# Flamingo gated block: another order of the first loads, of GpSimd's constants and of the first normalisation

## The chip, the cores and the metric

The kernel runs on one core of one Trainium2 chip. The metric is the device time of one execution in microseconds (us). The core has five engines that run their own instruction streams and meet in semaphores: TensorE (PE, with its weight loads PEld), VectorE (DVE), ScalarE (ACT), GpSimd (POOL) and SyncE (SP), which here only issues transfers. Transfers run on 16 DMA engines. SP's transfers are on queue q1, ACT's on queue q10.

## The reference

`x` is 32 batches of 56 tokens of 128 features; `ctx` is 32 batches of 1500 context rows of 128 features.

```python
x = x + tanh(g_xattn) * xattn(layernorm(x), ctx)     # 16 heads of depth 8, biases on q, k, v, o
x = x + tanh(g_ffn)   * ffn(layernorm(x))            # 160 experts, top 8 of sigmoid(logits), plus one shared

# xattn: q = xn@Wq.T+bq; k = ctx@Wk.T+bk; v = ctx@Wv.T+bv
#        out = softmax(q.k/sqrt(8)) @ v, per head;  out @ Wo.T + bo
# ffn:   p = sigmoid(xn@router.T + bias); top 8, normalised to sum 2.5
#        sum over experts of  silu(xn@w_gate[e].T) * weight[e] @ w_down[e].T
```

## The kernel before

**Attention.** Tokens are kept as `xt` [112, 16, 128]: two batches side by side on the partitions, 16 such pairs. The pairs fall in four groups of 448 tokens (`TC`); `FIRST` is the first group (pairs 0 to 3), `REST` the three others. Context rows of one batch are `ctx_in[:, u]` with 125 partitions of 12 rows, in three chunks of four tiles (`NCH = 3`); `u` is the batch's parity. For each chunk GpSimd makes a high and a low fp16 part (`split_ctx`, lines 563 and 565), SP issues a DMA transpose into `ctT` (line 377), PE makes the keys from it in three products (lines 1298 for batch 0, 1401 for the others), ACT writes the high part of the keys (733, 858) and DVE the low part (982, 1160). GpSimd builds from the queries `q_hi` a block matrix `q_blk` (line 663). PE multiplies it with the keys in 21 products a batch, which only give the row maxima (line 1377; DVE reduces each, line 1030; three PSUM banks hold them, so a product must wait for the maximum two places before it). The scores themselves come from stacked rows, `k_stk` and `q_st` (line 1358), ACT takes their exponential (line 800) and PE multiplies them with the values (line 1343).

**Steps.** `attention()` runs `body(step)` for each step on each engine; a body has 12 places k = 0 to 11. In step s the keys of batch s, the maxima and values of batch s-1 and the scores of batch s-2 are made. Keys come at k = 2, 6, 10 on PE, and one place later on ACT and DVE; values at k = 0, 4, 8 on PE and at k = 1, 5, 9 on ACT. Scores begin at k = 3. So step 1 has the maxima of batch 0 and the keys of batch 1, and step 2 has the first scores. Steps 0 to 3 are written out, the rest is a loop. What stands aside of this is put at places by tables such as `SCALE_REST_AT = (1, 3)` (step 1, k = 3), called by `aside`.

**Aside work that the change touches.** The layernorm of `FIRST` is made before step 1: DVE centres (`centre`, lines 953 to 955), ACT squares (709) and takes roots (718), DVE scales (967, 968), PE transposes four pairs (1277), ACT copies (723), PE multiplies with `wqT` (1292), ACT writes `q_hi` (728), DVE `q_lo` (976). The layernorm of `REST`: DVE `centre(*REST)` (953 to 955) before step 1, ACT `square_rest` (739), DVE variance (1005, `VAR_REST_AT`), ACT root (718), DVE reciprocal (1010, `RSTD_REST_AT`), ACT `scale_rest` (745, `SCALE_REST_AT`), then tokens (`TOKENS_REST_AT`), query products (`Q_REST_AT`), `q_hi` (`Q_HI_REST_AT`) and `q_lo` (`Q_LO_REST_AT`). The 16 rows of Wo, `output_rows`, are copied by 16 transfers that ACT issues in fours (line 789, `OUT_ROWS_AT`).

**Start.** SP issues the first tokens (line 330), chunk 0 of batch 0 (325), the four weights Wq, Wk, Wv, Wo (347), chunks 1 and 2. ACT issues the padding rows (749), three biases (752), the remaining tokens (330) and the rows of batch 1 (325). PE may begin with the transposes of the weights (1273) when all four are there; ACT copies these (761). After the three transposes of batch 0, SP has in its stream: load of batch 2, eight issues of `stack_queries` (369, after `q_hi` and `q_lo`), transpose of chunk 0 of batch 1, four issues more, chunks 1 and 2 of batch 1, `stack_keys` of batch 0 (405, 12 issues). GpSimd waits for the padding and splits the three chunks of batch 0, then makes its constants (608 to 617), then `q_blk`.

**FFN.** After attention a loop over 80 expert pairs runs on PE, ACT and DVE (lines 1540, 1550, 867, 874, 1203, 1210). The change touches nothing there.

Of the kernel before, what the change touches and what calls it, by code (L numbers as in the profile page):

```python
# [14 lines left out]
def flamingo_gated_block(nc, x, ctx, g_xattn, g_ffn, Wq, bq, Wk, bk, Wv, bv, Wo, bo,  # L15
# [53 lines left out]
    FIRST, REST = (0, PPC), (PPC, NP)  # L69
    VAR_REST_AT, RSTD_REST_AT, SCALE_REST_AT = (1, 1), (1, 2), (1, 3)  # L70
    TOKENS_REST_AT = {(1, 5): (1, 3), (1, 8): (3, 4)}
    Q_REST_AT = {(1, 6): (1, 3), (1, 9): (3, 4)}
    Q_HI_REST_AT = {(1, 7): (1, 3), (1, 10): (3, 4)}
    Q_LO_REST_AT = {(1, 8): (1, 3), (1, 11): (3, 4)}
    SHARED_AT, GATES_AT, CONSTANT_AT, QUERIES_FREE_AT, OUT_FREE_AT = (2, 0), (2, 1), (2, 2), (2, 1), (2, 4)
    OUT_ROWS_AT = {(1, 4): 0, (1, 6): 4, (1, 8): 8, (1, 10): 12}
    AGGR_AT = (B - 2, 2)
# [12 lines left out]
    with stk:  # L90
# [236 lines left out]
        def load_x(eng, p0, p1, here):  # L327

            for b in range(2):
                eng.dma_start(xt[b * T:(b + 1) * T, p0:p1, :],  # L330
                              x.rearrange("(n b) t c -> b t n c", b=2)[b, :, p0:p1, :]).then_inc(here, 16)
# [7 lines left out]
        def _(sp):  # L339
            def load_chunk(c):  # L340
                j = slice(c * TPC, (c + 1) * TPC)
                load_rows(sp, first_here[c], ctx_in[0:KP, 0, j, :], ctx[0].rearrange("(p j) c -> p j c", j=KT)[:, j, :])

            load_x(sp, *FIRST, x_in)
            load_chunk(0)
            for n, w in enumerate((Wq, Wk, Wv, Wo)):
                sp.dma_start(w_raw[:, n, :], w).then_inc(weights_in, 16)
            for c in range(1, NCH):
                load_chunk(c)
# [171 lines left out]
        def _(pool):  # L521
            made = [0]

            def const(ins):

                made[0] += 1
                ins.then_inc(consts, 1)
                pool.wait_ge(consts, made[0])
# [75 lines left out]

            pool.wait_ge(pad_here, 32)
            for c in range(NCH):
                split_ctx((0, 0), c)
            const(pool.memset(den_spread[:, :], 0.0))
# [5 lines left out]
            const(pool.memset(k_stk[96:97, 0, 0, :], 1.0))  # L614
            assert made[0] == K_ONES
            const(pool.memset(v_sb[:, :, :, 0:4, 3 * d:VW], 1.0))
            const(pool.memset(v_sb[:, :, :, 4:VG, d:VW], 1.0))
# [88 lines left out]
        def _(act):  # L706
# [41 lines left out]
            for u in range(2):  # L748
                act.dma_start(ctx_in[KP:128, u, :, :], ctx[0].rearrange("(p j) c -> p j c", j=KT)[0:128 - KP, :, :])\
                   .then_inc(pad_here, 16)  # L750
            for dst, src in ((bqc, bq), (bkc, bk), (bvc, bv)):
                act.dma_start(dst[:, :], src.rearrange("(p a) -> p a", a=1)).then_inc(bias_in, 16)
            load_x(act, *REST, x_rest)
            load_rows(act, ctx_here[1], ctx_in[0:KP, 1, :, :], ctx[1].rearrange("(p j) c -> p j c", j=KT))
            act.wait_ge(o_cleared, 2)
            load_root_table(1, sq_first[:, 0, 0:1], ones_d[0:PT, 0:1])
            square(1, sq_first, *FIRST)

            for n, w in enumerate((wqT, wk_hi, wv_hi, woT)):
# [178 lines left out]
        def _(dve):  # L938
# [53 lines left out]
            scale(1, *FIRST)  # L992
            dve.wait_ge(x_rest, 32)
            centre(*REST)
            dve.wait_ge(bias_in, 16 * 3)
            dve.wait_ge(bqs_made, 1)
            queries(0, 1)
            for c in range(NCH):
                first_keys(c)
            dve.wait_ge(o_cleared, 2)  # L1000
            v.tensor_scalar(bv_rep[:, :], ones_d[:, :], bvc[:, 0:1], None, ALU.mult).then_inc(bv_made, 1)
# [652 lines left out]
```

## Time and profile before

| | us |
|---|---|
| three runs | 1126.83, 1124.95, 1122.03 |
| median | 1124.95 |
| the profiled execution, its own time | 1124.83 |
| its span | 1123.2 |
| PE busy in the span | 1068.0 |
| DVE busy | 963.5 |
| ACT busy | 847.6 |
| GpSimd busy | 591.7 |

The mean granted clock of TensorE is 0.99 of full speed. The span counts from the first to the last instruction. PE is busy for 95% of it, except in its first 40th, 28 us, where it is busy for two tenths. The change touches the first 60 us alone.

### The profile page before, as it was taken

The page shows a single profiled execution, that of the slowest core. Times are in us where ns is not written, and L with a number is a line of the kernel's source. Part 1 is how long each engine was busy: PE and PEld are TensorE (multiplying, and loading weights), DVE is VectorE, ACT ScalarE, POOL GpSimd, SP SyncE. Part 2 cuts the span into 40 slices and gives each one's busy share as a digit, 9 for nine tenths or more (in the row PEclk, how much of TensorE's full clock was granted, in tenths as well). Part 3 has the DMA queues.
Part 4 walks back from the last instruction along what each step waited for, and adds up shares of the span by engine and source line. Part 5 has one row for each costly group of instructions (what it writes and reads, how often), then busy time and mean ns, then how long its engine had stood idle before and what let it go on. Part 6 is the DMA issues. An engine that isn't in the chain of part 4 may idle for free.

```text
span 1123.2 us, 37415 instructions
## 1 busy us (share of the span) xinstructions
PE 1068.0 (95%) x12142; PEld 708.1 (63%) x12142; DVE 963.5 (86%) x1699; ACT 847.6 (75%) x1817; POOL 591.7 (53%) x984
## 2 busy tenths in 40 slices
PE   2799999999999999999999999998999999999998
PEld 1366777777777777777777777654455555555554
DVE  4678888888888888888888888578999999999998
ACT  3476777777777777777777776687888888888887
POOL 5798887887888888788888886320000000000000
PEclk9799999999999999999999999999999999999999
DMA  8778777577577576676676652482788778777873
GB/s 159 158 166 214 145 178 179 123 184 170 133 186 170 131 186 162 142 185 152 152 185 142 150 132 67 110 207 97 229 228 226 226 236 237 229 229 227 230 237 118
DMA packets 229501, 197.12 MB, mean 175 GB/s; under 512 B 161039, under 2 KB 207263, under 8 KB 229462
## 3 DMA queue, kind: packets, MB, share of 16 engines
q1 hardware_dynamic: 218036, 173.22, 61.8%
q0 software_dynamic: 9200, 21.85, 6.9%
q10 hardware_dynamic: 2226, 1.56, 0.7%
q8 instruction: 21, 0.34, 0.1%
q14 instruction: 18, 0.15, 0.0%
HBM read 109.96 MB, written 12.55 MB: 109 GB/s over the span
## 4 chain that ended last, share of the span: by engine, by line
PE 75%; DVE 12%; issue 4%; SPq 3%; ACT 2%; DMA 2%; DVEq 0%; POOL 0%; ACTq 0%
PE bank L1550 15%; PE bank L1540 15%; PE bank L1343 12%; PE bank L1377 11%; PE bank L1358 10%; DVE part_max L1030 6%; PE bank L1413 5%; PE bank L1401 4%; DVE rec L1169 2%; PE bank L1457 1%; SPq L369 1%; DMA ctx_in<-in_ctx_dram 1%; SPq L405 1%; DVE o_raw L1044 1%; DVE kparts L1160 1%
## 5 line engine op out<-in xcount | busy, mean ns | idle before, releaser
L800 ACT ACTIVATE p_exp<-bank 125x448 f32<-125x448 f32 x768 | 400.1, 544 | 183.9 <-PE bank L1358 182.9
L1030 DVE TENSOR_REDUCE part_max<-bank 128x1 f32<-128x500 f32 x672 | 420.1, 671 | 62.0 <-PE bank L1377 61.5
L1358 PE MATMUL bank<-q_st,k_stk 97*125 97x224 f16 x1536 | 272.6, 261 | 2.5 <-ACT p_exp L800 1.9
L1377 PE MATMUL bank<-kparts,q_blk 128*128 128x500 f16 x672 | 255.8, 384 | 17.5 <-DVE part_max L1030 13.2
L1358 PEld LDWEIGHTS bank<-q_st,k_stk 97*125 97x125 f16 x1536 | 195.9, 138 | 66.2 <-ACT p_exp L800 13.1
L867 ACT ACTIVATE ctT<-bank 128x448 f32<-128x448 f32 x320 | 174.2, 545 | 40.9 <-DVE v_sb L1203 9.8
L1210 DVE TENSOR_TENSOR ctT<-v_sb,ctT 128x448 f16<-128x448 f32 (+1 forms) x324 | 200.4, 619 | 0.2
L1550 PE MATMUL bank<-ctT,w_ring 128*128 128x448 f16 x816 | 198.9, 352 | 0.1
L874 ACT ACTIVATE ctT<-v_sb 128x448 f16<-128x448 f32 x320 | 182.2, 569 | 7.0 <-DVE v_sb L1203 6.9
L1343 PE MATMUL bank<-p_exp,v_sb 125*25 125x168 f32 (+1 forms) x6144 | 186.2, 262 | 0.4 <-ACT p_exp L800 0.4
L1343 PEld LDWEIGHTS bank<-p_exp,v_sb 125*25 125x25 f32 x6144 | 142.1, 103 | 42.6 <-ACT p_exp L800 0.5
L1540 PE MATMUL bank<-q_hi,w_ring 128*128 128x448 f16 x544 | 147.3, 352 | 0.0
L1550 PEld LDWEIGHTS bank<-ctT,w_ring 128*128 128x128 f16 x816 | 79.7, 98 | 74.6 <-DVE ctT L1210 3.5
L565 POOL TENSOR_TENSOR ctx_parts<-ctx_in,ctx_parts 128x512 f16<-128x512 f32 x96 | 111.2, 1159 | 8.0
L1203 DVE TENSOR_TENSOR v_sb<-v_sb,ctT 128x448 f32<-128x448 f32 x154 | 95.8, 622 | 6.9 <-ACT ctT L867 2.6
L1203 DVE TENSOR_TENSOR v_sb<-k_stk,ctT 128x448 f32<-128x448 f32 x154 | 96.0, 624 | 5.6 <-issue 2.5
L1160 DVE SCALAR_TENSOR_TENSOR kparts<-bank,bkc,kparts 128x500 f16<-128x500 f32 x93 | 68.0, 731 | 38.0 <-ACT kparts L858 38.0
L1540 PE MATMUL bank<-q_lo,w_ring 128*128 128x448 f16 x272 | 95.9, 352 | 0.0
L1377 PEld LDWEIGHTS bank<-kparts,q_blk 128*128 128x128 f16 x672 | 64.9, 97 | 44.2 <-DVE part_max L1030 23.5
L1540 PEld LDWEIGHTS bank<-q_hi,w_ring 128*128 128x128 f16 x544 | 53.2, 98 | 49.7
L1413 PE MATMUL bank<-wv_hi,ctT 128*125 128x128 f16 x768 | 84.0, 224 | 0.0
L1413 PEld LDWEIGHTS bank<-wv_hi,ctT 128*125 128x125 f16 x768 | 77.7, 140 | 2.8 <-issue 2.8
(193 smaller groups left out, 1376.3 us busy)
## 6 DMA issues: line engine op xcount, KB each, us to landing
k_stk<-kparts SPq DMA_DIRECT2D x384, 93.8 KB, 4.1
v_sb<-c_scratch SPq DMA_DIRECT2D x68, 448.0 KB, 4.3
k_stk<-c_scratch SPq DMA_DIRECT2D x68, 448.0 KB, 4.3
ctx_in<-in_ctx_dram SPq DMA_DIRECT2D x30, 672.0 KB
w_scratch<-w_out POOLq DMA_DIRECT2D x80, 128.0 KB, 3.2
w_in<-in_L_ffn_w_gate_dram POOLq DMA_DIRECT2D x80, 64.0 KB, 3.7
w_in<-in_L_ffn_w_down_dram POOLq DMA_DIRECT2D x80, 64.0 KB, 4.1
v_sb<-c_scratch SPq DMA_DIRECT2D x8, 336.0 KB, 3.8
```

The source lines that it names most:

```text
L800: act.activation(p_exp[0:KP, j % PR, f * 448:(f + 1) * 448], ST[f][0:KP, 0:448], ACT.Exp).then_inc(exp_done, 1)
L867: act.activation(s_act[:, (r - 1) % 2 if isinstance(r, int) else z % 2, :], ZB[z][:, 0:TC], ACT.Silu)\
L874: act.activation(h_hi[:, b, :], h_f[:, b, :], ACT.Copy).then_inc(hh_done, 1)
L1030: v.reduce_max(part_max[:, i // NCH, i % NCH:i % NCH + 1], SM[i % NSM][:, 0:CK], axis=AX.X).then_inc(sm_maxed, 1)
L1203: v.tensor_tensor(h_f[:, b, :], c, s_act[:, (r - 1) % 2 if isinstance(r, int) else b % 2, :], ALU.mult).then_inc(h_done, 1)
L1210: v.tensor_tensor(h_lo[0:rows, b, :], h_f[0:rows, b, :], h_hi[0:rows, b, :], ALU.subtract).then_inc(hl_done, 1)
L1343: last = pe.matmul(OB[32 * (g % 4):32 * (g % 4) + VW, at:at + w], v_sb[0:KP, u, j, g, 0:VW], p_exp[0:KP, j % PR, src:src + w], start=(j == ...
L1358: last = pe.matmul(ST[f][0:KP, (g % 2) * GC:(g % 2 + 1) * GC], k_stk[0:97, u, g, j * KP:(j + 1) * KP], q_st[0:97, u, g, :, :].rearrange("p ...
L1377: pe.matmul(SM[i % NSM][:, 0:CK], rows, kparts[:, u, 0, c * CK:(c + 1) * CK], start=True, stop=True).then_inc(sm_done, 1)
L1413: last = pe.matmul(VB[0:KP, i * D:(i + 1) * D], ctT[:, u, c, part, i, 0:KP], w[:, :], start=(n == 0), stop=(n == 2))
L1540: last = pe.matmul(ZB[z][:, 0:TC], w[:, a, :], xparts[b][:, t * TC:(t + 1) * TC], start=(j == 0), stop=(j == 2))
L1550: last = pe.matmul(YB[t][:, 0:TC], part, hparts[b][rows, at, :], start=(shared and i == 0), stop=(end and i == 2), skip_group_check=True)
```

## The change

The weights are issued by ACT after the padding, in place of SP between chunks 0 and 1. ACT issues the remaining tokens and batch 1 behind `square(1, ...)`, no longer ahead of the table load. GpSimd makes `den_spread` and the ones of `k_stk` ahead of its wait for the padding; the two fills of `v_sb` stay behind the splits. DVE centres `REST` behind the first keys. The tables move the rest of that layernorm by three places, and the output rows to other places.

```diff
-    VAR_REST_AT, RSTD_REST_AT, SCALE_REST_AT = (1, 1), (1, 2), (1, 3)
-    TOKENS_REST_AT = {(1, 5): (1, 3), (1, 8): (3, 4)}
...
+    VAR_REST_AT, RSTD_REST_AT, SCALE_REST_AT = (1, 4), (1, 5), (1, 6)
+    TOKENS_REST_AT = {(1, 8): (1, 3), (1, 11): (3, 4)}
...
-    OUT_ROWS_AT = {(1, 4): 0, (1, 6): 4, (1, 8): 8, (1, 10): 12}
+    OUT_ROWS_AT = {(1, 1): 0, (1, 4): 4, (2, 0): 8, (2, 2): 12}
...
             load_x(sp, *FIRST, x_in)
-            load_chunk(0)
-            for n, w in enumerate((Wq, Wk, Wv, Wo)):
-                sp.dma_start(w_raw[:, n, :], w).then_inc(weights_in, 16)
-            for c in range(1, NCH):
+            for c in range(NCH):
                 load_chunk(c)
...
-            pool.wait_ge(pad_here, 32)
-            for c in range(NCH):
-                split_ctx((0, 0), c)
             const(pool.memset(den_spread[:, :], 0.0))
...
             const(pool.memset(k_stk[96:97, 0, 0, :], 1.0))
             assert made[0] == K_ONES
+            pool.wait_ge(pad_here, 32)
+            for c in range(NCH):
+                split_ctx((0, 0), c)
...
+            for n, w in enumerate((Wq, Wk, Wv, Wo)):
+                act.dma_start(w_raw[:, n, :], w).then_inc(weights_in, 16)
             for dst, src in ((bqc, bq), (bkc, bk), (bvc, bv)):
...
-            load_x(act, *REST, x_rest)
-            load_rows(act, ctx_here[1], ctx_in[0:KP, 1, :, :], ctx[1].rearrange("(p j) c -> p j c", j=KT))
             act.wait_ge(o_cleared, 2)
             load_root_table(1, sq_first[:, 0, 0:1], ones_d[0:PT, 0:1])
             square(1, sq_first, *FIRST)
+            load_x(act, *REST, x_rest)
+            load_rows(act, ctx_here[1], ctx_in[0:KP, 1, :, :], ctx[1].rearrange("(p j) c -> p j c", j=KT))
...
             scale(1, *FIRST)
-            dve.wait_ge(x_rest, 32)
-            centre(*REST)
...
             for c in range(NCH):
                 first_keys(c)
+            dve.wait_ge(x_rest, 32)
+            centre(*REST)
```

The tables of the query products move likewise: `Q_REST_AT` from (1, 6) and (1, 9) to (1, 9) and (2, 0), `Q_HI_REST_AT` from (1, 7) and (1, 10) to (1, 10) and (2, 0), `Q_LO_REST_AT` from (1, 8) and (1, 11) to (1, 11) and (2, 1). PE's wait `QUERIES_FREE_AT` goes from (2, 1) to (2, 2).

VectorE's stream before, from the scaling of the first tokens to the first maxima of step 1:

```order
L968 TENSOR_TENSOR xc<-xc,stat 112x512
L953 TENSOR_REDUCE stat<-xt 112x12
L954 TENSOR_SCALAR stat<-stat 112x12
L955 TENSOR_TENSOR xc<-xt,stat 112x1536
L976 SCALAR_TENSOR_TENSOR q_lo<-bank,bqs,q_hi 128x448
L982 SCALAR_TENSOR_TENSOR kparts<-bank,bkc,kparts 128x500 x3
L1001 TENSOR_SCALAR bv_rep<-ones_d,bvc 128x112
L1030 TENSOR_REDUCE part_max<-bank 128x1 x4
```

The same place in the changed kernel:

```order
L967 TENSOR_TENSOR xc<-xc,stat 112x512
L975 SCALAR_TENSOR_TENSOR q_lo<-bank,bqs,q_hi 128x448
L981 SCALAR_TENSOR_TENSOR kparts<-bank,bkc,kparts 128x500 x3
L952 TENSOR_REDUCE stat<-xt 112x12
L953 TENSOR_SCALAR stat<-stat 112x12
L954 TENSOR_TENSOR xc<-xt,stat 112x1536
L1000 TENSOR_SCALAR bv_rep<-ones_d,bvc 128x112
L1029 TENSOR_REDUCE part_max<-bank 128x1 x8
```

The three centring instructions of `REST` stand now between the last low part of the keys and the first maximum.

ScalarE's stream before, from the last keys of step 1 backwards and forwards to the first exponential (`xnT` are copies of tokens, `wo_m` the output rows):

```order
L789 DMA wo_m<-woT 8x128 x4
L834 ACTIVATE v_sb<-bank 125x4x4x24
L836 ACTIVATE v_sb<-bank 125x4x4x8
L728 ACTIVATE q_hi<-bank,bqs 128x448
L789 DMA wo_m<-woT 8x128 x4
L858 ACTIVATE kparts<-bank,bkc 128x500
L847 ACTIVATE neg_row<-bank 7x128
L834 ACTIVATE v_sb<-bank 125x4x4x24
L836 ACTIVATE v_sb<-bank 125x4x4x8
L776 ACT_TABLE_LOAD
L776 ACTIVATE tg<-g_raw 112x2
```

The same stretch in the changed kernel, from the last keys of step 1:

```order
L857 ACTIVATE kparts<-bank,bkc 128x500
L720 ACTIVATE xnT<-bank 128x448
L846 ACTIVATE neg_row<-bank 7x128
L725 ACTIVATE q_hi<-bank,bqs 128x448
L788 DMA wo_m<-woT 8x128 x4
L833 ACTIVATE v_sb<-bank 125x4x4x24
L835 ACTIVATE v_sb<-bank 125x4x4x8
L775 ACT_TABLE_LOAD
L775 ACTIVATE tg<-g_raw 112x2
L778 ACTIVATE sg<-bank 128x64
```

Eight of the output rows' issues leave step 1 for step 2, four of them right behind the last `q_hi` and four between the table load and the first exponential.

## Rows read from the trace of the kernel before

**Rows 1.** Chain of waits, first 110 us: start us, us, what.

```profile
6.37 12.10 DMA ctx_in<-in_ctx_dram
...
28.90 3.79 DMA ctT<-ctx_parts
...
75.27 0.79 SPq L413
```

**Rows 2.** Issues: source, queue, count, KB each, us to landing, for Wo.

```profile
w_raw<-in_L_xattn_Wo_dram SPq DMA_DIRECT2D x1, 64.0 KB, 7.7
```

**Rows 3.** Timeline of ScalarE: start us, us, instruction, idle before it.

```profile
4.38 1.28 ACTq L325 DMA_DIRECT2D ctx_in<-in_ctx_dram  x2
5.69 1.28 ACT L713 ACT_TABLE_LOAD   x1 [5.69 <-issue]
...
12.48 0.28 ACT L761 ACTIVATE wqT<-bank 128x128 f32<-128x128 f32 x1 [4.62 <-PE bank L1273]
...
22.04 0.63 ACT L728 ACTIVATE q_hi<-bank,bqs 128x448 f16<-128x448 f32 x1 [0.88 <-PE bank L1292]
...
47.12 2.72 ACTq L789 DMA_DIRECT2D wo_m<-woT  x4
49.89 0.49 ACT L834 ACTIVATE v_sb<-bank 125x384 f32<-125x384 f32 x1 [2.28 <-issue]
...
52.69 0.68 ACT L858 ACTIVATE kparts<-bank,bkc 128x500 f16<-128x500 f32 x1 [1.62 <-issue]
...
56.45 1.28 ACT L776 ACT_TABLE_LOAD   x1
...
60.25 0.54 ACT L800 ACTIVATE p_exp<-bank 125x448 f32<-125x448 f32 x1 [1.84 <-PE bank L1358]
```

**Rows 4.** Timeline of GpSimd.

```profile
5.99 0.61 POOL L563 CAST ctx_parts<-ctx_in 128x512 f16<-128x512 f32 x1 [2.44 <-DMA ctx_in<-in_ctx_dram]
...
25.31 1.68 POOL L663 TENSOR_TENSOR q_blk<-q_hi,head_mask 128x896 f16<-128x896 f16 x1
26.93 0.61 POOL L563 CAST ctx_parts<-ctx_in 128x512 f16<-128x512 f32 x1
...
28.72 0.61 POOL L563 CAST ctx_parts<-ctx_in 128x512 f16<-128x512 f32 x1
```

**Rows 5.** Timeline of SP's issues.

```profile
23.71 2.55 SPq L369 DMA_DIRECT2D q_stk<-q_hi  x4
```

**Rows 6.** Timeline of TensorE.

```profile
19.02 0.60 PE L1298 MATMUL bank<-ctT,wk_hi 128*128 128x500 f16 x1 [3.47 <-DMA ctT<-ctx_parts]
...
53.47 0.99 PE L1377 MATMUL bank<-kparts,q_blk 128*128 128x500 f16 x2 [2.49 <-issue]
```

**Rows 7.** Windows: busy of PE, PEld, DVE, ACT, POOL; granted clock, DMA share, GB/s.

```profile
4.00:6.00 2.00, 0.00 (x0) 0.00 (x0) 1.45 (x3) 0.31 (x1) 0.01 (x1) 1.00 0.54 135
...
8.00:10.00 2.00, 0.00 (x0) 0.00 (x0) 0.74 (x2) 0.00 (x0) 0.00 (x0) 1.00 1.18 201
...
44.00:46.00 2.00, 0.06 (x1) 0.00 (x0) 2.00 (x5) 0.02 (x1) 2.00 (x4) 1.00 0.51 156
46.00:48.00 2.00, 1.94 (x7) 1.25 (x8) 1.02 (x2) 0.54 (x1) 2.00 (x4) 0.52 0.61 171
```

**Rows 8.** Timeline of VectorE.

```profile
15.33 1.75 DVE L953 TENSOR_REDUCE stat<-xt 112x12 f32<-112x1536 f32 x1 [0.91 <-DMA xt<-in_x_dram]
...
17.83 1.76 DVE L955 TENSOR_TENSOR xc<-xt,stat 112x1536 f32<-112x1536 f32 x1
```

**Rows 9.** Groups by line, 26 to 53 us, VectorE: busy us, mean ns, idle before.

```profile
L1030 DVE TENSOR_REDUCE part_max<-bank 128x1 f32<-128x500 f32 x21 | 13.2, 672 | 7.8 <-PE bank L1377 7.8
```

**Rows 10.** Groups by line, 30 to 60 us, ScalarE.

```profile
L745 ACT ACTIVATE xc<-xc,stat 112x128 f32<-112x128 f32 x12 | 3.6, 390 | 0.0
```

**Rows 11.** Groups by line, 44 to 52 us, TensorE.

```profile
L1292 PE MATMUL bank<-xnT,wqT 128*128 128x448 f32 x2 | 1.9, 1034 | 0.0
...
L1277 PE MATMUL bank<-ident,xc 112*128 112x112 f32 x4 | 1.0, 398 | 2.0 <-DVE q_lo L976 2.0
```

More of the change, by code:

```diff
@@ L69, in flamingo_gated_block @@
     FIRST, REST = (0, PPC), (PPC, NP)
-    VAR_REST_AT, RSTD_REST_AT, SCALE_REST_AT = (1, 1), (1, 2), (1, 3)
-    TOKENS_REST_AT = {(1, 5): (1, 3), (1, 8): (3, 4)}
[L72 to L75, printed above, removed]
-    OUT_ROWS_AT = {(1, 4): 0, (1, 6): 4, (1, 8): 8, (1, 10): 12}
+    VAR_REST_AT, RSTD_REST_AT, SCALE_REST_AT = (1, 4), (1, 5), (1, 6)
+    TOKENS_REST_AT = {(1, 8): (1, 3), (1, 11): (3, 4)}
+    Q_REST_AT = {(1, 9): (1, 3), (2, 0): (3, 4)}
+    Q_HI_REST_AT = {(1, 10): (1, 3), (2, 0): (3, 4)}
+    Q_LO_REST_AT = {(1, 11): (1, 3), (2, 1): (3, 4)}
+    SHARED_AT, GATES_AT, CONSTANT_AT, QUERIES_FREE_AT, OUT_FREE_AT = (2, 0), (2, 1), (2, 2), (2, 2), (2, 4)
+    OUT_ROWS_AT = {(1, 1): 0, (1, 4): 4, (2, 0): 8, (2, 2): 12}
     AGGR_AT = (B - 2, 2)
```

## The prediction, made before the changed kernel was run

> **What bounds the kernel now.** I read the chain of waits of the first 110 us, then the timelines of the engines over 60 us, then windows of 2 us for the clock and the transfers. PE is busy for 95% of the span, so most of the time can't be touched here; but in the first 28 us it is busy for a fifth. There the chain is one transfer, 12.10 us long [rows 1]: the last chunk of batch 0, behind weights, other tokens and batch 1. TensorE's first keys start at 19.02, after 3.47 us of waiting for the transpose [rows 6], which lay in SP's queue behind all chunks. `q_hi` of the first group ends at 22.04 + 0.63 = 22.67 [rows 3]. From there SP issues eight stacks of queries (23.71 on, 0.64 each) and at 28.90 the transpose of batch 1's chunk 0, which lands 3.79 later, at 32.7 [rows 1, 5]. GpSimd begins `q_blk` only at 25.31, though `q_hi` is there 2.6 us before [rows 4]: its constants are in the way. Step 2 starts on PE at 53.47, after 2.49 us without a wait that the profile shows [rows 6]; ScalarE's last keys were late, as its engine sat idle 1.62 us while its stream issued four output rows, and 2.28 us before that [rows 3]. The first exponential starts at 60.25 [rows 3]. From there the work is bound by PE, SP's row of maxima follows at 75.27 [rows 1] and all that comes later hangs on it. So I follow one quantity: how much earlier than 60.25 the first exponential starts. Nothing behind it is changed, and I count that gain one for one in the span.
>
> **The start.** What is needed first is 224 KB of tokens, 768 KB of batch 0 with its padding and 256 KB of weights, 1.28 MB. Data flow from about 2 us, at 135 GB/s in 4:6 and 201 in 8:10 [rows 7]; my sum over the windows puts 1.28 MB at 8.6 to 8.8 (all earlier tokens and rows of batch 1 are out of the way). The weights are the last of it or ahead: Wo landed 7.7 us after its issue [rows 2], near 11.9; now at 8.6. PE's transposes take about 1.1, ACT's copies begin at 9.75 in place of 12.48 [rows 3]. ACT has by then issued the four transfers that move behind `square`: the table load stays within 0.6 of its 5.69 [rows 3] (four weights' issues come ahead of it, four others go), the square ends near 7.3, issues of 2.3 us (1.28 for batch 1's two [rows 3], 1.0 for the tokens) run from 6.9 to 9.2, free. The normalised first tokens are 2.7 earlier, at 12.85 on PE. The transpose of chunk 0 is issued as now at about 7.9, since the split starts at 5.99 [rows 4] after chunk 0's landing, and with 3.79 to land is there at 11.7; a bound on the other side is 13. The first keys start at 12.85 in place of 19.02, and `q_hi` ends 3.65 later as now, at 16.5: 6.2 earlier. GpSimd's early constants fit in the 2.44 us for which it waits now [rows 4]; if chunk 0 lands before they are done, they cost at most 0.5. A split takes 1.79 (26.93 to 28.72 [rows 4]), so the third ends at 11.4, its transpose lands at 15.2 to 16.4, and the third low part of the keys ends near 18.7.
>
> **What takes the place.** (a) `centre(*REST)` now stands between the keys and the maxima: 15.33 to 19.59, 4.26 us [rows 8]. First maximum at 23.3. Six maxima at 13.2/21 = 0.63 [rows 9] end at 27; PE's keys at k = 2 need only the fourth, 25.1. So the centring, once hidden behind the wait for the transfer, is hidden again, behind SP. (b) SP: 16.5 plus 5.2 of issues is 21.7. But batch 1 must be here and split: its rows and the other tokens are 1.45 MB and begin to flow at 9.2; at 201 GB/s [rows 7] that is 16.4, and three transposes of 0.25 MB each beside it make it 20.2. Split 1.79, transpose at 22.0, landing at 25.85 in place of 32.7: 6.8 earlier. The bounds of the landing are 25.5 (SP alone) and, below as a rival, 29 or more.
>
> (c) Step 1 behind that. Before: 32.7 to 53.47, 20.8 us. Now ScalarE's work comes in series, since the scaling of `REST` is at k = 6 behind the second four output rows. The terms: keys of batch 1 1.45; two maxima, a low part, two maxima, variance and root 3.6; four issues 2.72 (the stream of ScalarE is held, as the 2.28 of idle shows [rows 3]), behind which stand values, scaling and the second keys; values 0.75; scaling 3.6 [rows 10]. VectorE waits for the second keys then, and PE stands idle for some 2.7 us. An idle of 2 us in 44:46 is followed by a granted clock of 0.52, the lower level, in 46:48 [rows 7], so I take the tokens at 1.0 a group and the first query product at 1.9 [rows 11]: two groups of tokens 2.0; maxima between 0.9; queries 1.9 and 0.9; last maximum and keys 0.9; ACT's keys 0.7; low parts 0.7 and 0.6; the last tokens 0.9. Sum 21.6, so step 2 starts at 47.45, 6.0 earlier. The old idle from the output rows ahead of the last keys is gone, but the serial scaling and the clock eat it.
>
> (d) Head of step 2. Before: 53.47 to 60.25, 6.8. Now two maxima and the values 2.2; the last query product, which moved in here, 1.9 at the lower clock (0.9 at the higher); then ACT, in order: `q_hi` and four issues 2.7, values 0.75, to 55.0; the table load (1.28, begun at 56.45 before [rows 3]) with its copies, and beside it four more issues, 2.1 more. First exponential at 57.1 in place of 60.25. VectorE's constant term waits for the same copies and stays beside it. That costs 2.9 of the 6.0: eight output rows stand where the first scores are wanted. If the clock is at its higher level here, 1.2 less.
>
> The sum: 6.8 gained up to the landing, 0.8 lost in step 1, 2.9 lost in the head of step 2: 3.1 to 3.2 earlier. The profiled execution took 1124.83, and the median of the runs shown is 1124.95, the same within 0.1. Forecast 1121.6. Its own range is 1119.8 (higher clock in both places, SP's bound) to 1123.
>
> SP's and GpSimd's streams keep up: SP reaches the row of maxima of batch 0 near 48, 6 to 7 earlier than at present, and the scores want it at 54.
>
> **Rivals.**
> 1. The whole gain of the head survives. The output rows' issues have cost idle time before as well, and if PE keeps its higher clock (in 44:46 it was still 1.00 [rows 7]) and ScalarE issues the last four beside its queued work, step 2 starts at 46 and the first exponential is bound by PE's scores alone, 6.8 to 7.5 later: 53.3, 6.9 gained, 1117.9. Against: the 2.28 and 1.62 of idle [rows 3] say the issues do hold the engine.
> 2. Batch 1 comes last; this is the way to slower. SP loads batch 2 (0.77 MB) right behind the third transpose, at 12.7, beside ACT's queue. If the 16 engines serve the two in turn, 1.45 + 0.75 + 0.77 = 2.97 MB must pass: at 201 GB/s to 24.0, at 135 [rows 7] to 31. It decides from 20.0 on, and each microsecond later is one lost on GpSimd's split, SP's transpose and everything queued behind it. At 24.0: 3.8 more, 1125.4; at 26, 1127.4; at 31, 1132. For it: the twelve-microsecond transfer of [rows 1] was such a mixture. Against: 2.7 MB passed by 16 us in the kernel before.
> 3. The weights don't come earlier: behind another queue Wo may again take until 11.9 [rows 2], since batch 0's three chunks now run beside them. Then copies at 12.5 and all from the first keys on is 2.7 later: 1124.3. This is also how the change would not do what it says.
>
> On rival 2 the Trainium skill speaks. "DMA: Bandwidth & Descriptors", section "Queues, rings and completion order", says that each DMA engine takes turns between the queues with work, a packet at a time, and its section "Issuing engines are not separate DMA queues" that issuing from two engines saves only issue time. By that rule batch 1 would share evenly with batch 2 from about 14.7 and land near 22.5; the sum would be 2.3 us less gain, 1123.9. The trace agrees as far as it shows it, for q10's tokens were issued by 4.4 and landed only at 15.33, beside q1's weights and chunks.
>
> **How the numbers follow.** Forecast 0.48; rival 1 0.27; rival 2 0.15; rival 3 0.10. Range: 1117.0, below rival 1, to 1125.6, which takes in rivals 3 and the milder half of 2; about 0.1 is left above and 0.08 below. A measurement of this kernel can tell some 0.5%, 5.6 us, from no change. Faster by more than that is below 1119.3: rival 1 nearly whole and a little of the forecast, 0.31. Slower by more is above 1130.6: only the far end of rival 2, 0.05. Within: 0.64.
>
> **What would show it.** ACT's weight copies near 9.8 and `q_hi` ending near 16.5 (rival 3: 19). The first maximum on VectorE near 23.3, behind the centring. The first wait for keys in step 1 ending at 25 to 26 (rival 2: GpSimd waits for batch 1's rows beyond 20). Step 2 at 47 to 48. ScalarE idle for "issue" ahead of the first exponential, which starts at 57 (rival 1: 53), and a granted clock near 0.5 ahead of it. The prediction is wrong if the span behind the first exponential, 1123.2 less 60.25, should become longer or shorter by more than 1 us.

## The result, and the profile after

The changed kernel took 1130.11 us, the median of 7 runs (1127.82 to 1149.86), against 1124.06 of the kernel before (7 runs, 1122.03 to 1127.24). The run of 1149.86 had a lower granted clock than the six others (0.941 against 0.988 to 0.991), so the ratio leaves it out; the median of the six is 1129.06. The ratio is 1.0048, with a 95% interval of 1.0027 to 1.0069: slower by about half a per cent, some 5 us. The forecast was 1121.6, its range 1117.0 to 1125.6; the time lies outside it, on the slow side.

The profiled execution took 1132.42, with a span of 1130.9, 7.7 more than before. It was the slowest of the six, so the losses read from it are some 2 us larger than those of the medians. Four marks in the two traces say where it went. The first is the start of the first keys of batch 1 on TensorE, the second the start of step 2, the third the first exponential, the fourth SP's row of maxima [rows 1].

| mark | before | forecast | after |
| --- | --- | --- | --- |
| first keys of batch 1 | 32.7 | 25.85 | 32.08 |
| step 2 | 53.47 | 47.45 | 53.47 |
| first exponential | 60.25 | 57.1 | 64.64 |
| SP's next row of maxima | 75.27 | | 81.60 |
| end of the span | 1123.2 | | 1130.9 |

So 0.7 us were gained up to batch 1, lost again in step 1, 4.4 were lost in the head of step 2, 1.9 in the 15 us behind the first exponential, and 1.4 in the thousand behind those. TensorE's timeline of the changed kernel (start us, us, instruction, idle ahead of it in brackets) answers to [rows 6]:

```profile
8.23 1.09 PE L1272 MATMUL bank<-ident,w_raw 128*128 128x128 f32 x4 [8.23 <-DMA w_raw<-in_L_xattn_Wo_dram]
...
17.50 0.60 PE L1297 MATMUL bank<-ctT,wk_hi 128*128 128x500 f16 x1 [5.33 <-DMA ctT<-ctx_parts]
...
30.52 1.77 PE L1376 MATMUL bank<-kparts,q_blk 128*128 128x500 f16 x3 [4.53 <-DVE part_max L1029]
32.08 0.62 PE L1400 MATMUL bank<-ctT,wk_hi 128*128 128x500 f16 x1
...
44.22 1.76 PE L1276 MATMUL bank<-ident,xc 112*128 112x112 f32 x8 [2.58 <-ACT xc L742]
...
53.47 1.04 PE L1376 MATMUL bank<-kparts,q_blk 128*128 128x500 f16 x2
...
60.19 0.38 PE L1357 MATMUL bank<-q_st,k_stk 97*125 97x224 f16 x2 [0.20 <-issue]
...
65.23 0.63 PE L1357 MATMUL bank<-q_st,k_stk 97*125 97x224 f16 x2 [4.04 <-ACT p_exp L799]
```

The weights are earlier, as forecast (8.23). The first keys are only 1.5 us earlier than before, behind a wait of 5.33 for the transpose. At 30.52 TensorE waits for VectorE's maxima, no longer for a transfer. And the first scores of step 2 are ready near 60.6 but ScalarE takes them at 64.64; from 65.2 to 69.7 the matmuls that took 0.38 at 60.19 take about 0.6. The chain of waits (start, us, what) shows the new head, in answer to [rows 1]:

```profile
8.24 9.21 DMA ctT<-ctx_parts
17.50 1.43 PE bank L1297 x3
18.93 1.51 PE bank L1291 x2
20.52 0.64 ACT q_hi L725
```

One transfer of 12.10 us has been replaced by a transpose of 9.21. It is the first of batch 0's three; why it is so long, e4 and e9 show. VectorE's timeline, in answer to [rows 8]:

```profile
24.27 1.74 DVE L952 TENSOR_REDUCE stat<-xt 112x12 f32<-112x1536 f32 x1
26.05 0.54 DVE L953 TENSOR_SCALAR stat<-stat 112x12 f32<-112x12 f32 x1
26.62 2.10 DVE L954 TENSOR_TENSOR xc<-xt,stat 112x1536 f32<-112x1536 f32 x1
28.65 1.22 DVE L1000 TENSOR_SCALAR bv_rep<-ones_d,bvc 128x112 f32<-128x112 f32 x1
29.80 3.59 DVE L1029 TENSOR_REDUCE part_max<-bank 128x1 f32<-128x500 f32 x6
...
44.76 0.74 DVE L1159 SCALAR_TENSOR_TENSOR kparts<-bank,bkc,kparts 128x500 f16<-128x500 f32 x1 [3.93 <-ACT kparts L857]
```

The centring stands ahead of the first maximum without a gap, and that maximum is at 29.80. Later VectorE waits 3.93 for keys that ScalarE gives late. ScalarE's timeline says why, in answer to [rows 3]:

```profile
8.77 0.28 ACT L760 ACTIVATE wqT<-bank 128x128 f32<-128x128 f32 x1 [1.32 <-PE bank L1272]
...
20.52 0.63 ACT L725 ACTIVATE q_hi<-bank,bqs 128x448 f16<-128x448 f32 x1 [0.88 <-PE bank L1291]
...
37.34 2.63 ACTq L788 DMA_DIRECT2D wo_m<-woT  x4
40.02 0.49 ACT L833 ACTIVATE v_sb<-bank 125x384 f32<-125x384 f32 x1 [2.53 <-issue]
...
40.56 3.60 ACT L742 ACTIVATE xc<-xc,stat 112x128 f32<-112x128 f32 x12
44.06 0.66 ACT L857 ACTIVATE kparts<-bank,bkc 128x500 f16<-128x500 f32 x1
...
57.26 2.62 ACTq L788 DMA_DIRECT2D wo_m<-woT  x4
59.93 0.49 ACT L833 ACTIVATE v_sb<-bank 125x384 f32<-125x384 f32 x1 [2.09 <-issue]
...
60.60 1.28 ACT L775 ACT_TABLE_LOAD   x1
...
64.64 0.54 ACT L799 ACTIVATE p_exp<-bank 125x448 f32<-125x448 f32 x1 [2.08 <-issue]
```

Four issues, then twelve scalings, then the keys: the series that the new tables set up. In the head of step 2 the engine idles 2.09 and 2.08 us while its stream issues eight output rows, the second time with the scores waiting.

### The profile page after: what moved, and what is told of

Read it like the earlier page. It is cut to its first block, busy times and chain, and to the rows that moved or that the text cites. A ratio compares the mean times of both kernels' runs of the same rounds, so it can differ in the third digit from the quotient of the medians.

```text
span 1130.9 us, 37415 instructions
## 1 busy us (share of the span) xinstructions
PE 1071.3 (95%) x12142; PEld 709.8 (63%) x12142; DVE 965.9 (85%) x1699; ACT 847.8 (75%) x1817; POOL 593.7 (52%) x984
## 3 DMA queue, kind: packets, MB, share of 16 engines
q1 hardware_dynamic: 217460, 172.96, 60.6%
## 4 chain that ended last, share of the span: by engine, by line
PE 68%; DVE 15%; issue 6%; SPq 3%; POOL 3%; DMA 2%; ACT 2%; DVEq 1%; ACTq 0%; POOLq 0%
PE bank L1549 15%; PE bank L1539 15%; PE bank L1342 10%; PE bank L1357 9%; PE bank L1376 8%; DVE part_max L1029 8%; PE bank L1412 4%; DVE rec L1168 4%; PE bank L1400 3%; PE bank L1456 1%; SPq L402 1%; DMA ctT<-ctx_parts 1%; DVE o_raw L1043 1%; POOL ctx_parts L562 1%; DVE kparts L1159 1%
## 5 line engine op out<-in xcount | busy, mean ns | idle before, releaser
L1376 PE MATMUL bank<-kparts,q_blk 128*128 128x500 f16 x672 | 255.9, 383 | 20.3 <-DVE part_max L1029 18.7
```

The source lines that it names most:

```text
L1376: pe.matmul(SM[i % NSM][:, 0:CK], rows, kparts[:, u, 0, c * CK:(c + 1) * CK], start=True, stop=True).then_inc(sm_done, 1)
```

## The experiments

Each kernel was timed with the kernel before on the same chip; e1 to e4, e5 to e8 and e9 to e11 are three such groups, and across groups the ratios compare better than the medians. Keys, maximum, exponential and row are starts in the profiled execution: first keys on TensorE, first maximum on VectorE, first exponential, and SP's row at 75.27 before.

| kernel | median us | ratio to before, 95% | keys | maximum | exponential | row |
| --- | --- | --- | --- | --- | --- | --- |
| before | 1124.06 | 1 | 19.02 | 27.68 | 60.25 | 75.27 |
| changed | 1130.11 | 1.0048 [1.0027, 1.0069] | 17.50 | 29.80 | 64.64 | 81.60 |
| e1 | 1127.85 | 1.0033 [1.0020, 1.0046] | 17.61 | 29.90 | 62.37 | 78.00 |
| e2 | 1121.83 | 0.9979 [0.9969, 0.9989] | 17.10 | 24.41 | 56.86 | 71.87 |
| e3 | 1124.60 | 1.0003 [0.9990, 1.0016] | 18.14 | 28.05 | 58.70 | 73.72 |
| e4 | 1132.85 | 1.0081 [1.0060, 1.0101] | 11.72 | 33.63 | 67.50 | 84.36 |
| e5 | 1127.54 | 1.0032 [1.0017, 1.0047] | 17.35 | 24.63 | 60.27 | 77.42 |
| e6 | 1125.74 | 1.0017 [1.0006, 1.0027] | 17.46 | 24.72 | 60.15 | 77.62 |
| e7 | 1121.27 | 0.9974 [0.9961, 0.9986] | 17.39 | 24.86 | 56.37 | 71.39 |
| e8 | 1121.79 | 0.9974 [0.9962, 0.9985] | 17.13 | 24.41 | 56.85 | 72.39 |
| e9 | 1120.00 | 0.9965 [0.9952, 0.9977] | 14.43 | 21.68 | 54.17 | 69.72 |
| e10 | 1122.25 | 0.9982 [0.9968, 0.9996] | 17.22 | 26.28 | 56.33 | 71.35 |
| e11 | 1121.94 | 0.9982 [0.9970, 0.9994] | 14.43 | 23.90 | 53.55 | 68.93 |

**e1: the changed kernel with the output rows issued where they were.**

```diff
-    OUT_ROWS_AT = {(1, 1): 0, (1, 4): 4, (2, 0): 8, (2, 2): 12}
+    OUT_ROWS_AT = {(1, 4): 0, (1, 6): 4, (1, 8): 8, (1, 10): 12}
```

> The changed kernel with the 16 output rows at their old places (1, 4), (1, 6), (1, 8), (1, 10). Theory A (the issues of the output rows stand in front of the first exponentials of step 2, ScalarE idle 2.09 and 2.08 us for issue, PE idle 4.04 and then at half clock): the first exponential starts 3 to 4.5 us earlier than in the changed kernel (60 to 61.5 in place of 64.64), PE no longer drops to half clock behind it, total 1124 to 1126. Rival B (the loss is made in step 1, by the centring ahead of the maxima and the serial scaling; the rows only fill slack): the first exponential moves by under 1.5 us, since the issues in step 1 delay the keys there as much, total 1128 to 1131.

The first exponential comes 2.3 us earlier than in the changed kernel, bound by TensorE and not by issues; ScalarE's timeline in this kernel:

```profile
62.37 0.54 ACT L799 ACTIVATE p_exp<-bank 125x448 f32<-125x448 f32 x1 [0.26 <-PE bank L1357]
```

In time the difference is smaller and not clear of noise: the ratios 1.0048 and 1.0033 are 1.7 us apart, and e1's lies within the interval of the changed kernel. If it is real, the eight rows in the head of step 2 account for about a third of the loss; most of the loss is elsewhere.

**e2, e3, e7: the parts of the change that touch no table.** e2 is the kernel before with the new order of loads only, e3 with GpSimd's constants ahead of the splits only, e7 with both.

```diff
 # e2: in the kernel before
             load_x(sp, *FIRST, x_in)
-            load_chunk(0)
-            for n, w in enumerate((Wq, Wk, Wv, Wo)):
-                sp.dma_start(w_raw[:, n, :], w).then_inc(weights_in, 16)
-            for c in range(1, NCH):
+            for c in range(NCH):
                 load_chunk(c)
...
             square(1, sq_first, *FIRST)
+            load_x(act, *REST, x_rest)
+            load_rows(act, ctx_here[1], ...)
```

> The kernel before with only the new order of the loads (weights on ACT's queue, other tokens and batch 1 issued behind the square); centring, tables and GpSimd's constants as before. Theory A (the loads gain what they can, and the moved work costs it): the centring lies in VectorE's idle time ahead of the first keys, the first keys start near 17.5 as in the changed kernel, first maximum near 24.5 to 25.5 in place of 27.7, first exponential 1.5 to 3 us earlier than 60.25, total 1121 to 1123. Rival C (the loads themselves are the harm, as the transposes of batch 0 now share the DMA engines with batch 1): transposes and the keys of batch 1 come later than before, total 1126 or more.

> The kernel before with only GpSimd's constants (den_spread, ones of k_stk) ahead of its wait. Theory A: q_blk starts near 23.2 in place of 25.31, the first maximum is then bound by the third keys at 26, so 1.0 to 1.5 us earlier; the keys of batch 1 still wait for SP until 32.7, so the first exponential and the total move by 0 to 0.5: 1123.5 to 1124.5. Rival D (GpSimd is on the path in the start): 1.5 to 2.5 us earlier.

> The kernel before with the new loads and GpSimd's early constants; centring, tables, output rows as before. The run with the loads alone gave 1121.83. GpSimd finished the splits at 12.1 in the changed kernel and q_hi came at 21.2, so the constants are hidden there in either place: both theories expect no difference, 1121.3 to 1122.3; a gain over 1 us would say that GpSimd is on the path.

The loads alone make the kernel faster, 0.9979, with the interval below 1; the constants alone do nothing measurable (1.0003), and beside the loads they add nothing that the intervals part (0.9974). The loads are worth 2.4 to 3 us; the loss is in what came with them. e3's exponential is 1.5 us earlier than the kernel before's without a difference in the medians. Most likely that is how far one profiled execution scatters in this head (e3's took 1.1 us less than its median), so a difference of that size between two traces shows nothing.

**e6, e5: the changed kernel without the later centring, and with or without the new output rows.** e6 puts both back, so that it is e7 with the changed tables (variance, root, scaling, tokens and queries of the rest three places later); e5 puts back the centring alone. The edit of the centring is shown; that of the rows is e1's.

```diff
 # e5 and e6
+            dve.wait_ge(x_rest, 32)
+            centre(*REST)
             dve.wait_ge(bias_in, 16 * 3)
             dve.wait_ge(bqs_made, 1)
             queries(0, 1)
             for c in range(NCH):
                 first_keys(c)
-            dve.wait_ge(x_rest, 32)
-            centre(*REST)
```

> The changed kernel with centre(*REST) back at its place before, ahead of the first keys; tables and output rows as changed. Theory G (the centring ahead of the first maximum is the largest part of the loss): the first maximum starts near 24.5 in place of 29.80; but the tables still put ScalarE's scaling at k = 6 behind four issues, so the first exponential is 2 to 4 us earlier than 64.64, total 1125 to 1128. Rival H (step 1 is set by the serial chain of the tables and SP, the centring lies beside it): under 1 us, total 1129 to 1131.

> The changed kernel with centre(*REST) and the output rows back; only the tables of the remaining layernorm stay moved by three places. If the three costs add (tables, centring, output rows), this is what the tables alone cost over the kernel with new loads and constants: theory G expects 1123 to 1124.5, that is 1 to 3 us above that kernel; rival H expects 1125 to 1127, the tables being the larger part.

The tables are the largest loss: e6 is 4.5 us above e7 in the medians (intervals 1.0006 to 1.0027 and 0.9961 to 0.9986), and its first exponential is 3.8 later though batch 1's keys start at the same time in both (29.45 and 29.39). ScalarE's timeline of e6:

```profile
35.41 0.21 ACT L715 ACTIVATE stat<-stat 112x12 f32<-112x12 f32 x1 [3.82 <-DVE stat L1004]
35.48 3.10 ACTq L788 DMA_DIRECT2D wo_m<-woT  x4
38.63 0.49 ACT L833 ACTIVATE v_sb<-bank 125x384 f32<-125x384 f32 x1 [3.00 <-issue]
```

and TensorE's:

```profile
42.83 1.76 PE L1276 MATMUL bank<-ident,xc 112*128 112x112 f32 x8 [2.58 <-ACT xc L742]
...
52.59 0.98 PE L1276 MATMUL bank<-ident,xc 112*128 112x112 f32 x4 [4.03 <-DVE q_lo L975]
```

The root waits for a late variance, the values wait for four issues, the tokens for the scaling; the first tokens of the rest come at 42.83, against 34.70 in e7, and the last at 52.59 against 42.32. Nothing is left ahead of the scores to hide that.

Why the old places cost less shows in ScalarE's timeline of the kernel before:

```profile
34.97 0.76 ACTq L789 DMA_DIRECT2D wo_m<-woT  x1
35.07 0.97 ACT L745 ACTIVATE xc<-xc,stat 112x128 f32<-112x128 f32 x3
```

There four issues, from 34.97 to 37.72, stand right behind the twelve scalings. The stream has gone ahead to the issues while the engine still works through the scalings, which take 3.6 us (34.78 to 38.37) as without any issue beside them. With the changed tables the four issues at (1, 4) stand ahead of the scalings, behind a short root alone, and the engine idles 2.53 us (changed kernel) or 3.00 (e6) for them.

The centring costs e1 against e6 1.8 us by the ratios, 1.0033 against 1.0017; the two intervals overlap a little, so the traces must carry it: the first maximum is 5.2 later, batch 1's first keys 2.7 (32.18 and 29.45), the first exponential 2.2. The same edit with the new rows, e5 against the changed kernel, has the first maximum 5.2 and the exponential 4.4 apart, and again overlapping ratios, 1.0032 and 1.0048. The output rows (e5 against e6) change the medians by 1.8, with overlapping intervals, and in the traces the first exponential not at all. They only change what it waits for, as TensorE's timeline of e5 shows:

```profile
55.84 0.38 PE L1357 MATMUL bank<-q_st,k_stk 97*125 97x224 f16 x2 [0.20 <-issue]
...
60.86 0.63 PE L1357 MATMUL bank<-q_st,k_stk 97*125 97x224 f16 x2 [4.03 <-ACT p_exp L799]
```

Step 1 without the last eight rows is shorter, the scores are there 3.9 us before e6's, and ScalarE then takes them at 60.27 all the same, since it issues the eight rows first. With the early centring the issues are paid in the one place or in the other.

**e4: the changed kernel with batch 1 and the other tokens held back until the first tokens are on ScalarE (about 12 us).**

```diff
-            load_x(act, *REST, x_rest)
-            load_rows(act, ctx_here[1], ...)
...
             query_tokens(0, 1)
+            load_rows(act, ctx_here[1], ...)
+            load_x(act, *REST, x_rest)
             first_keys(0)
```

> The changed kernel with batch 1's rows and then the other tokens issued by ACT behind the first tokens' copy (near 12.8 us in place of 6.8 to 8.7). Theory E (the first transpose took 9.2 us to land, from 8.24, because those 1.45 MB pass the same DMA engines beside it): it lands within 3 to 4.5 us, first keys at 12.3 to 13, q_hi ends near 16; but batch 1 is here only at 22 to 25 and the centring waits for the other tokens, so the total is open, 1122 to 1132. Rival F (the first transposes are slow by themselves so early, whatever runs beside them): it lands near 17.4 again and the keys start no earlier than 17.

This is the experiment on the first transpose. TensorE's timeline:

```profile
11.72 0.60 PE L1297 MATMUL bank<-ctT,wk_hi 128*128 128x500 f16 x1
...
21.46 0.60 PE L1297 MATMUL bank<-ctT,wk_hi 128*128 128x500 f16 x1 [5.89 <-DMA ctT<-ctx_parts]
```

Issued at 8.51, the first transpose is there by 11.72, with no wait shown: at most 3.2 us, where the changed kernel's took 9.2. The windows of the two kernels (busy of PE, PEld, DVE, ACT, POOL; granted clock, DMA share, GB/s) show what lay beside it. First e4:

```profile
8.00:10.00 2.00, 1.04 (x4) 0.64 (x4) 1.40 (x6) 1.10 (x6) 1.92 (x3) 1.00 0.09 17
```

then the changed kernel:

```profile
8.00:10.00 2.00, 1.09 (x4) 0.71 (x4) 1.40 (x6) 1.04 (x6) 1.92 (x4) 1.00 0.86 217
10.00:12.00 2.00, 0.81 (x4) 0.66 (x4) 1.04 (x1) 0.00 (x0) 1.92 (x2) 1.00 1.16 177
```

The engines were free for it in e4 and full of the other tokens and batch 1 in the changed kernel. But the kernel is slower, 1.0081: the held loads then lie beside the third transpose (the wait of 5.89 at 21.46), and the other tokens arrive only at 27.57, so the centring and with it the first maximum, at 33.63, come later still. Contention is moved, not taken away.

**e8, e9: on top of e7, output rows in ScalarE's idle time; then batch 1 issued by SP behind batch 0's transposes.**

```diff
 # e8, in e7
-    OUT_ROWS_AT = {(1, 4): 0, (1, 6): 4, (1, 8): 8, (1, 10): 12}
+    OUT_ROWS_AT = {(1, 1): 8, (1, 4): 12}
...
             query_tokens(0, 1)
+            output_rows(0, 8)
             first_keys(0)
 # e9, in e8
-            load_rows(act, ctx_here[1], ...)
...
+            load_rows(sp, ctx_here[1], ...)
             load_ctx((0, 0))
```

> New loads and early constants, centring and tables as before, and the output rows where ScalarE waits anyway: eight issues behind the first tokens' copy (12.9 us, ahead of a wait of some 5.7 us for the first keys), four at (1, 1), four at (1, 4). Theory A (an issue in ScalarE's stream costs time where work is queued behind it): the idle 'issue' of 2.2, 2.8 and 1.6 us in step 1 is gone, step 2 starts 1.6 to 3 us earlier than with the loads alone, total 1119 to 1120.5. Rival I (step 1 is bound by SP and VectorE, ScalarE's idle time costs nothing): no gain, 1121.5 to 1122.3.

> The kernel with output rows in ScalarE's idle time, and batch 1's rows issued by SP behind the three transposes of batch 0, so that only the other tokens (0.69 MB) pass beside the first transpose. Theory E: the first transpose lands in 5 to 6.5 us in place of 8, first keys near 14.5 in place of 17.1, q_hi 2 to 2.5 us earlier; SP's stacks follow, unless batch 1 is late; batch 1's chunk 0 is bound by its rows, 1 to 2 us earlier than 29; total 1119.5 to 1121.5. Rival F (the first transpose is slow whatever runs beside it): keys at 17 again.

e8's eight issues from 12.63 on are free, and step 2 starts at 47.61, against e7's 49.36; but nothing comes of it (both 0.9974). TensorE's timeline of e8:

```profile
54.17 0.60 PE L1401 MATMUL bank<-ctT,wk_hi 128*128 128x500 f16 x1 [3.09 <-DMA ctT<-ctx_parts]
...
56.21 0.61 PE L1358 MATMUL bank<-q_st,k_stk 97*125 97x224 f16 x2 [0.60 <-DMA q_st<-neg_row]
```

What is late next are the transposes of batch 2 and the row of maxima, both in SP's queue. In e9 the whole head moves:

```profile
14.43 0.60 PE L1298 MATMUL bank<-ctT,wk_hi 128*128 128x500 f16 x1 [2.83 <-DMA ctT<-ctx_parts]
...
26.71 0.60 PE L1401 MATMUL bank<-ctT,wk_hi 128*128 128x500 f16 x1 [2.75 <-DMA ctT<-ctx_parts]
```

With only the other tokens (0.69 MB) beside it, the first transpose is there at 14.4, 6.2 us after its issue at 8.23: between the 3.2 of e4 and the 9.2 of the changed kernel, and in the order of the bytes beside it. What the bytes set is the moment, more than the time from the issue: in the changed kernel, e1, e2, e5 to e8 and e10 the transpose is issued at 8.23 to 9.19, and the first keys start at 17.1 to 17.6 all the same; in e9 and e11 it is issued at 8.23 and 9.36, and they start at 14.43 in both. The first exponential is at 54.17. e9 is the fastest version found, 1120.0 us, 0.9965 [0.9952, 0.9977], faster than the kernel before and than the changed one; that it beats e7 (0.9974) its interval doesn't show.

**e10, e11: SP's seven small inputs issued by ScalarE in the same idle time, on e8 and on e9.**

```diff
-            small_inputs()                     # on SP, behind the keys of step 1
...
             query_tokens(0, 1)
+            small_inputs()                     # the same seven transfers, on ScalarE
+            output_rows(0, 4)
             first_keys(0)
-    OUT_ROWS_AT = {(1, 1): 8, (1, 4): 12}
+    OUT_ROWS_AT = {(1, 1): 4, (1, 4): 8, (1, 7): 12}
```

> The kernel with output rows in ScalarE's idle time, with SP's seven small inputs issued by ScalarE in the same idle time (the last four rows go to (1, 7)). There step 2 started at 47.6, but PE then waited 3.1 us for batch 2's first transpose and 0.6 for the row of maxima, both in SP's stream behind these inputs (41.06 to 44.74). Theory J (SP's stream bounds the head of step 2 there): SP is 3.7 us earlier, the first exponential at 53 to 54 in place of 56.85, total 1117 to 1119. Rival K (the transposes are held by the DMA engines, not by SP's stream): no gain, 1121 to 1122.

> Both of the other two kernels' edits together: batch 1 on SP behind the transposes, small inputs on ScalarE's queue. If theories E and J both hold the gains add in part: total 1116 to 1118.5; if the rows of batch 1 become the bound, as the kernel with small inputs on ScalarE alone or slower.

Neither gains: 1122.25 and 1121.94, both 0.9982. SP has its issues back, but ScalarE has four output rows more in step 1, and its keys wait for them again; its timeline in e10:

```profile
29.83 2.63 ACTq L760 DMA_DIRECT2D wo_m<-woT  x4
32.52 0.68 ACT L858 ACTIVATE kparts<-bank,bkc 128x500 f16<-128x500 f32 x1 [2.53 <-issue]
```

Their first maxima are also later, 26.28 against e8's 24.41 and 23.90 against e9's 21.68. TensorE's wait for batch 2's transpose (3.09 us in e8, 3.05 in e9) is gone in both, but their step 2 also starts 3.3 and 3.9 us later. So these two runs don't tell whether SP's stream alone limits step 2, since the cure loads the other stream. That stays open. A kernel with the output rows off both queues wasn't tried.

## Why the prediction was wrong, step by step

**The start.** The weights came as forecast and a little earlier: copies at 8.77, forecast 9.75, and rival 3 (weights no earlier) is out. The step that failed is the next one, "with 3.79 to land is there at 11.7; a bound on the other side is 13". It landed at 17.45, outside my own bounds. I took the duration from a transpose of batch 1 [rows 1], which ran when the loads were over, and put it where the other tokens and batch 1 were issued from 6.83 to 8.7, just ahead of it. Without those loads beside it the transpose takes at most 3.2 (e4), with them 9.2. The kernel before had shown it: its transposes up to 60 us, from issue to landing, are

```profile
DMA to landing us min/median/max: 3.0/3.8/11.0
```

and the 11.0 is this same first transpose, issued at 7.92 and used at 19.02 [rows 6]. I put its lateness down to its place in SP's queue and took the median for it. And (b) charges batch 1's load with the bytes of the transposes that pass beside it, but never the transposes with the bytes of the load. So `q_hi` ended at 21.15 and not at 16.5, 1.5 us earlier than before instead of 6.2.

On this the prediction had the right rule and used it in the wrong place. It cited the Trainium skill, "DMA: Bandwidth & Descriptors", section "Queues, rings and completion order", that the DMA engines take turns between queues, for batch 1 against batch 2 alone (rival 2). The landings of 3.2, 6.2 and 9.2 us by what passed beside them fit the rule, though no trace shows the turns themselves; but what suffered was the small transfer on which everything hung, not batch 1's rows. GpSimd's timeline of the changed kernel shows those were there in time:

```profile
21.30 1.68 POOL L660 TENSOR_TENSOR q_blk<-q_hi,head_mask 128x896 f16<-128x896 f16 x1 [7.44 <-ACT q_hi L725]
22.93 0.61 POOL L560 CAST ctx_parts<-ctx_in 128x512 f16<-128x512 f32 x1
```

It begins batch 1's split right behind `q_blk`, without a wait for a transfer. Rival 2 as I wrote it didn't happen. SP issued the queries from 21.18 and batch 1's transpose at 26.36, 2.5 earlier than before, as its 5.2 of issues said.

**(a) The centring** was not hidden. I had it end at 23.3 behind keys that came at 18.7, and SP's transpose at 25.85 cover it. In fact it began at 24.27, ended with `bv_rep` 5.5 us later instead of 4.6, and the first maximum at 29.80 held TensorE 4.53 us. The sum had left it no room either: at 0.63 a maximum the fourth ends at 25.8, not at 25.1, against SP's 25.85. e6 and e1 price it at about 2 us.

**(b) Batch 1's first keys** started at 32.08, forecast 25.85. By there 6.2 us are lost of the 10.9 between forecast and profile (a span of 1130.9, against 1123.2 less 3.15). e5, e6 and e7, which centre early, start these keys at 29.4 to 29.7, so some 3.7 of the 6.2 belong to the landing and 2.5 to the centring. The others are -0.2 in step 1, 1.5 in the head of step 2 and 3.3 behind the first exponential.

**(c) Step 1** was right in size: 21.4 us, forecast 21.6, with the serial scaling (3.60 behind four issues of 2.63), VectorE's wait and the lower clock as described. What the account lacked is the comparison that matters. It charged this step with 0.8 of loss because the kernel before took 20.8 from a later start. e7, with the old tables behind the same loads, takes 20.0 to the start of step 2, with the last query product in it; e6 shows that the tables cost 3.8 us at the first exponential and 4.5 in the median. So the late landing explains why the gain was small, and the tables, the centring and the rows why it turned into a loss: with the same late landing e7 takes 1121.27.

**(d) The head of step 2** took 11.17 us, forecast 9.65, before 6.78. The mechanism was right (eight issues ahead of the first exponential, idle for "issue" twice). The size was short by 1.5. Up to the end of the first values it was even shorter than forecast, 7.1 us into the step against 7.55. But from the table load to the exponential I took 2.1, with the last four issues beside the load; they came behind it and its first copy, at 61.96, so this piece is 1.3 of load and 2.7 of issues in series, 4.04 us from 60.60 to 64.64. I had no bound for the case that they stand in series.

**Behind the first exponential** I said that nothing changes, with 1 us as the mark of error. It was 3.3. TensorE had stood idle for 4.04 us with two pairs of scores done and ScalarE late, and the windows of the changed kernel show the clock after it:

```profile
62.00:64.00 2.00, 0.00 (x0) 0.00 (x0) 1.16 (x6) 0.56 (x4) 1.70 (x4) 0.91 1.03 195
64.00:66.00 2.00, 0.77 (x3) 0.40 (x3) 1.37 (x4) 1.36 (x3) 1.92 (x3) 0.50 1.03 277
66.00:68.00 2.00, 2.00 (x13) 1.54 (x13) 1.78 (x3) 1.16 (x3) 1.62 (x6) 0.50 1.19 216
68.00:70.00 2.00, 2.00 (x19) 1.41 (x21) 0.61 (x2) 1.02 (x4) 2.00 (x4) 0.50 1.18 147
```

The granted clock is at 0.50, the lower of its two levels (1.2 and 2.4 GHz), for the first 5 us of a stretch that is bound by TensorE. e1, which has no such wait, keeps the higher one there; its windows:

```profile
64.00:66.00 2.00, 1.56 (x18) 1.27 (x19) 2.00 (x5) 0.89 (x2) 2.00 (x4) 1.00 1.01 187
66.00:68.00 2.00, 2.00 (x41) 1.47 (x40) 1.99 (x4) 1.59 (x5) 1.85 (x4) 1.00 1.08 324
```

From the first exponential to SP's row it is 15.0 to 15.6 us in the kernel before and in e1 to e3 and e7 to e11, and 16.9 to 17.5 in the changed kernel and in e4, e5 and e6. In all four of the second kind the windows show a granted clock of 0.50 for some 3 to 6 us within the stretch. In the first kind it is at 1.00, or 0.95 in one window, but for e8 and e9, where 0.50 lasts some 2.6 us into the stretch and the stretch takes 15.5. In the changed kernel, e4 and e5 the wait of 4 us stands ahead of the fall; in e6 the clock fell behind shorter waits, of 0.38 and 0.81 us, so what else sets it is open. From that row on all kernels run alike as far as two rows on: the next but one row of maxima comes 42.5 to 43.6 us later.

The step "I count that gain one for one in the span" held where the clock stayed up: in the profiled executions of e2, e3 and e7 to e11 the span is shorter than before by the gain at the first exponential less 0.2 to 1.1 us. It failed where the clock fell: e5 and e6 have their first exponential when the kernel before has it, and spans 2.8 and 1.8 longer. The medians follow less closely: e11's exponential is 6.7 us earlier, its span 5.6 shorter, and its ratio of 0.9982 is 2.0 us.

Rival 1 (the whole head gain of 6.9 survives, 1117.9) didn't happen in this kernel, but it can be had in part: e9 has its first exponential 6.1 earlier, at 54.17, once the transpose is relieved and the tables are left alone, and is 3.9 us faster by its ratio. The chances were badly set as well. A time between the range's end, 1125.6, and 1130.6, where 1130.11 lies, had only some 0.05, and slower than that another 0.05, all of it on one transfer, though the prediction itself listed three places (serial scaling, centring ahead of the maxima, eight issues ahead of the scores) in which the change makes the path longer and only one, the landing, in which it makes it shorter.

## What to carry to other kernels

Price a small transfer that everything waits for by what is in flight beside it, not by its duration in a quiet stretch: with bulk loads issued from another queue just ahead of it, it took 6 us longer here. When loads are brought forward, time the loads alone before moving anything behind them: here they were worth 2.4 to 3 us, and what was moved along with them lost some 8, the tables alone 4.5. Put issues of transfers behind work that the engine still has queued, not ahead of it. Where a stretch that is bound by TensorE follows a wait of some 4 us on it, look at the granted clock behind the wait: in the three kernels here with such a wait right ahead of the stretch it was the lower one, and the stretch took some 2 us longer.

## What was unexpected in the hardware

- The first transpose by DMA took at most 3.2 us with a DMA share of 0.09 around it (e4), 6.2 beside 0.69 MB (e9), and 9.2 beside 1.45 MB (changed kernel); the loads issued ahead of it differ. e8 and e9 are the clean pair: with batch 1's 0.77 MB moved behind the transposes alone, the landing goes from 8.0 to 6.2 us after the issue and the first keys from 17.13 to 14.43.
- VectorE and GpSimd held each other up. The centring's subtraction took 2.10 us beside GpSimd's split in the changed kernel, e1 and e4, 2.72 in e3, and 1.76 in the nine others. In one of these, the kernel before [rows 8], it was GpSimd that paid: the first half of a split that began within the subtraction, at 18.52, took 1.53 instead of 0.61. `bv_rep` took 1.22, in the kernel before 0.40. GpSimd's timeline of the changed kernel has the other side there too, the second half of a split at 2.60 beside them and at 1.15 just before:

```profile
25.41 1.15 POOL L562 TENSOR_TENSOR ctx_parts<-ctx_in,ctx_parts 128x512 f16<-128x512 f32 x1
...
27.20 2.60 POOL L562 TENSOR_TENSOR ctx_parts<-ctx_in,ctx_parts 128x512 f16<-128x512 f32 x1
```

  The times fit that the later of the two waits for the earlier one's end: the subtraction ends at 28.72, 1.15 more is 29.87, and the split's half ends at 29.80. No run here tests that by itself.

- An issue of 4 KB took ScalarE's stream 0.6 to 0.8 us wherever it stood: four took 2.63 here, 2.72 before [rows 3], and eight took 5.39 in e8, where nothing waited. It holds the stream and not the engine: the scalings of the kernel before went on beside four issues. It costs time when the engine has nothing queued.
